# Splitting the top-k search of a 16-expert MoE layer into two groups of eight, the second one run beside the experts

## What is computed

```python
scores = sigmoid(h @ gate_w.T)                       # 2048 x 16, h = layernorm(x1)
cap = ceil(T / E * 2)                                # 256
topk_score, topk_ids = top_k(scores.T, cap)          # per expert: the 256 best tokens
xin = h[topk_ids]
up = einsum(xin, up_w) + up_b; g = einsum(xin, gw) + gb
eo = einsum(silu(g) * up, down_w) + down_b           # hidden width 512
out = zeros.at[topk_ids].add(eo * topk_score)
shared = (silu(x @ sh_gate_w.T) * (x @ sh_up_w.T)) @ sh_down_w.T
return x + out + shared
```

## Time and profile before

| | us |
|---|---|
| median of three runs | 240.09 |
| the three runs | 242.76, 240.09, 237.68 |
| the profiled execution | 242.11 |
| its span | 240.4 |
| PE busy | 195.7 (81%) |
| DVE busy | 129.5 (54%) |
| POOL busy | 105.2 (44%) |
| ACT busy | 76.1 (32%) |
| mean granted TensorE clock | 0.921 |

### The profile page before, as it was taken

How to read it: one execution, slowest core, us unless ns; L and a number is a source line. 1 busy time by engine, 2 the same in 40 slices (tenths; PEclk the granted TensorE clock), 3 DMA queues, 4 the chain that set the end, 5 groups by cost and what they waited for, 6 DMA issues and landing times.

```text
span 240.4 us, 3505 instructions
## 1 busy us (share of the span) xinstructions
PE 195.7 (81%) x1256; PEld 163.0 (68%) x1256; DVE 129.5 (54%) x383; ACT 76.1 (32%) x177; POOL 105.2 (44%) x109
## 2 busy tenths in 40 slices
PE   7579999999697789954979499999999888879100
PEld 7455697999563456543858489989998777769000
DVE  3779167399719999985732434444444443334000
ACT  1475111325955000100021334444444334334100
POOL 7500034146300000000577267877788777635660
PEclk9957999999999999996599979999999999999855
DMA  6999992000008301101042033333233323312331
GB/s 203 387 419 419 414 417 115 3 1 3 1 0 252 121 0 44 46 0 44 17 105 61 14 46 37 46 38 45 37 46 46 50 38 45 26 20 22 24 30 11
DMA packets 11585, 22.20 MB, mean 92 GB/s; under 512 B 1456, under 2 KB 8752, under 8 KB 11440
## 3 DMA queue, kind: packets, MB, share of 16 engines
q1 hardware_dynamic: 5936, 17.52, 19.1%
q0 software_dynamic: 5632, 4.46, 14.3%
HBM read 17.65 MB, written 4.33 MB: 91 GB/s over the span
## 4 chain that ended last, share of the span: by engine, by line
PE 41%; POOL 17%; DVE 13%; DMA 12%; issue 10%; ACT 2%; POOLq 1%; SPq 0%
POOL out_dram L413 10%; DMA out_dram<-area,rows 8%; POOL hT L401 6%; PE bank L1185 5%; PE bank L1186 4%; PE bank L1019 4%; PE bank L1169 4%; PE bank L899 4%; PE bank L920 4%; PE bank L1063 3%; DMA x_tok<-in_x_dram 3%; DVE stats L551 2%; POOL rstd L378 2%; DVE area L746 2%; PE bank L1028 2%
## 5 line engine op out<-in xcount | busy, mean ns | idle before, releaser
L413 POOL DMA_INDIRECT out_dram<-area,rows x32 | 50.8, 1587 | 26.1 <-DMA out_dram<-area,rows 13.0
L401 POOL DMA_INDIRECT hT<-h_rows,rows x32 | 32.5, 1017 | 59.8 <-DVE rows L825 50.3
L530 ACT ACTIVATE sgate<-bank,consts 128x256 f32<-128x256 f32 x64 | 29.9, 469 | 70.9 <-PE bank L1186 60.2
L867 DVE SCALAR_TENSOR_TENSOR area<-bank,consts,sgate 128x256 f32<-128x256 f32 x64 | 30.8, 482 | 39.3 <-ACT sgate L530 32.3
L1185 PE MATMUL bank<-area,wT 128*128 128x256 f32 x128 | 40.1, 395 | 7.7 <-issue 7.0
L1169 PEld LDWEIGHTS bank<-wT,area 128*128 128x128 f32 x256 | 38.6, 193 | 4.2 <-issue 0.9
L1169 PE MATMUL bank<-wT,area 128*128 128x128 f32 x256 | 39.2, 278 | 0.5 <-issue 0.5
L1186 PE MATMUL bank<-area,wT 128*128 128x256 f32 x128 | 38.5, 383 | 0.0
L1186 PEld LDWEIGHTS bank<-area,wT 128*128 128x128 f32 x128 | 24.6, 192 | 3.5
L1185 PEld LDWEIGHTS bank<-area,wT 128*128 128x128 f32 x128 | 19.7, 195 | 10.3 <-issue 9.1
L378 POOL TENSOR_TENSOR rstd<-var_eps,half_pow 128x4 f32<-128x4 f32 (+1 forms) x10 | 12.5, 1249 | 20.7 <-DVE var_eps L556 20.7
(11 more groups left out here) (156 smaller groups left out, 246.8 us busy)
## 6 DMA issues: line engine op xcount, KB each, us to landing
wT<-in_weights_dram SPq DMA_DIRECT2D x16, 768.0 KB, 17.3
h_rows<-hrow SPq DMA_DIRECT2D x2, 576.0 KB, 4.3
x_tok<-in_x_dram SPq DMA_DIRECT2D x2, 512.0 KB, 4.7
x_tok<-in_down_b_dram SPq DMA_DIRECT2D x1, 1024.0 KB, 7.7
out_dram<-x SPq DMA_DIRECT2D x4, 256.0 KB, 2.4
hT<-h_rows,rows POOLq DMA_INDIRECT x32
out_dram<-area,rows POOLq DMA_INDIRECT x32
sh_wT<-in_shared_dram SPq DMA_DIRECT2D x1, 384.0 KB, 6.5
```

The source lines that it names most:

```text
L401: pool.indirect_dma_start(out=gath[:, e % GBUF, c, :], out_offset=None, in_=h_rows[:, :], in_offset=bass.IndirectOffsetOnAxis(ap=rows[:, g ...
L413: pool.indirect_dma_start(out=out_rows, in_=eo[:, e % 2, c, :], in_offset=None, out_offset=bass.IndirectOffsetOnAxis(ap=rows[:, g, c, k:k ...
L530: act.activation(sgate_e[:, q % SGB, :], up_bank(q)[:, CAP:2 * CAP], ACT.Silu, bias=biasT[:, 1, j, e:e + 1]).then_inc(s_sil, 1)
L867: dve.scalar_tensor_tensor(hidden[:, e % 2, j, :], up_bank(q)[:, 0:CAP], biasT[:, 0, j, e:e + 1], sgate_e[:, q % SGB, :], ALU.add, ALU.mul ...
```

## The change

The search, the ranks, the slots and the table are written as functions of a group g of eight experts, with buffers and semaphores of their own for each group (the second group's lie in `diag`, `attn_tok` and bank 7). Group 0 is searched first, with half as many elements in each compare (two of 448), and eight matmuls for a count, since one matmul now takes two tiles; an extra reduction (`total`) adds the two halves. Group 1 is searched later. Its compares are one instruction of 896 elements. Two of its ten rounds stand between `rows[0]` and expert 0, the other eight after the even steps q = 0 to 14; masks, ranks, slots, one-hots and table follow at steps 15 to 24. The shared expert's pieces are dealt out anew: PE does twelve products of them between `positions` and `table`. Bank 7 leaves the up banks, of which four are left. POOL gathers experts 0 to 5 ahead, 6 and 7 before scatters 1 and 2, none before scatters 3 and 4, then 8 and 9 together before scatter 5, and one before each scatter up to the eleventh.

```diff
--- before.py
+++ after.py
-        UP_BANKS = [bank[i] for i in (0, 1, 2, 6, 7)]
+        UP_BANKS = [bank[i] for i in (0, 1, 2, 6)]
...
+        PARTS = (((0, NT // 2), (NT // 2, NT)), ((0, NT),))
+        COUNTS = (bank[5], bank[7])
...
-            for e in range(GBUF - 1):
-                gather(e)
+            got = 0
             for e in range(E):
-                if e + GBUF - 1 < E:
-                    gather(e + GBUF - 1)
+                wanted = e + GBUF if e <= 2 else 8 if e < 5 else min(E, e + 5)
+                for n in range(got, wanted):
+                    gather(n)
+                got = wanted
                 scatter(e)
...
+            def high_keys(g):
+                dve.tensor_scalar(cand[g][:, :, :], ktab[:, :, 0:G], float(1 << ROUNDS[0]), None, ALU.mult)
+                dve.memset(thr[g][:, :], 0.0)
+                link(dve.tensor_scalar(by_tile(bits[g][:, 0, :]), score_bits(g), LOW, None, ALU.arith_shift_right))
+                link(dve.tensor_copy(key[g][:, 0, :], bits[g][:, 0, :]))
+            def low_keys(g):
+                link(dve.tensor_scalar(by_tile(bits[g][:, 1, :]), score_bits(g), (1 << LOW) - 1, None, ALU.bitwise_and))
+                mark(dve.tensor_scalar(key[g][:, 1, :], bits[g][:, 1, :], 1.0, None, ALU.add))
+            def compare(g, r):
+                bit = ROUNDS[r]
+                keys = key[g][:, 2 * (r // len(DIGITS)), :]
+                for i0, i1 in PARTS[g]:
+                    at_c = slice(i0 * G, i1 * G)
+                    dve.tensor_tensor(cmp[g][:, :, at_c].rearrange("p k (i e) -> p k i e", e=G),
+                                      by_tile(keys[:, at_c]).unsqueeze(1).to_broadcast([P, NC, i1 - i0, G]),
+                                      cand[g][:, :, :].unsqueeze(2).to_broadcast([P, NC, i1 - i0, G]),
+                                      ALU.is_ge).then_inc(s_cnt[g], 1)
+                if bit:
+                    dve.wait_ge(s_dve, step[0])
+                    mark(dve.scalar_tensor_tensor(base[g][:, :, :], ktab[:, :, 0:G], float(1 << (bit - 3)),
+                                                  per_expert(thr[g][:, :], NC), ALU.mult, ALU.add))
+            def decide(g, r):
+                bit = ROUNDS[r]
+                dve.wait_ge(s_tot[g], r + 1)
+                link(dve.tensor_reduce(total[g][:, :, :],
+                                       COUNTS[g][:, 0:2 * NC * G].rearrange("p (k s e) -> p k e s", k=NC, s=2), AX.X, ALU.add))
+                link(dve.tensor_scalar(met[g][:, :, :], total[g][:, :, :], float(CAP), float(1 << bit), ALU.is_ge, ALU.mult))
+                link(dve.tensor_reduce(gain[g][:, :], met[g][:, :, :].rearrange("p k e -> p e k"), AX.X, ALU.add))
+                if bit:
+                    n_cand = mark(dve.tensor_tensor(cand[g][:, :, :], per_expert(gain[g][:, :], NC), base[g][:, :, :], ALU.add))
+                    mark(dve.tensor_tensor(thr[g][:, :], thr[g][:, :], gain[g][:, :], ALU.add))
+                    dve.wait_ge(s_dve, n_cand)
+                else:
+                    link(dve.tensor_tensor(thr16[g][:, :], thr[g][:, :], gain[g][:, :], ALU.add))
+                if r == len(DIGITS) - 1:
+                    link(dve.tensor_tensor(above[g][:, :, :], by_tile(key[g][:, 0, :]), per_expert(thr16[g][:, :], NT),
+                                           ALU.subtract))
+                    dve.memset(thr[g][:, :], 1.0)
+                    dve.tensor_scalar(cand[g][:, :, :], ktab[:, :, 0:G], float(1 << ROUNDS[0]), 1.0, ALU.mult, ALU.add)
+                    link(dve.scalar_tensor_tensor(ranked[g][:, :, :], above[g][:, :, :], MARK, by_tile(key[g][:, 1, :]),
+                                                  ALU.mult, ALU.add))
+                    link(dve.tensor_scalar(by_tile(key[g][:, 2, :]), ranked[g][:, :, :], 0.0, MARK, ALU.max, ALU.min))
+            def masks(g):
+                for x, op in enumerate((ALU.is_gt, ALU.is_equal)):
+                    last = dve.tensor_tensor(by_tile(mask[g][:, x, :]), by_tile(key[g][:, 2, :]),
+                                             per_expert(thr16[g][:, :], NT), op)
+                link(last)
...
+            def slots(g):
+                dve.wait_ge(s_pos[g], 1)
+                dve.scalar_tensor_tensor(rank[g][:, 0, :], COUNTS[g][:, 0:P], -UNSET, mask[g][:, 0, :], ALU.add, ALU.mult)
+                link(dve.tensor_tensor(by_tile(rank[g][:, 1, :]), by_tile(COUNTS[g][:, P:2 * P]),
+                                       per_expert(above_no[g][:, :], NT), ALU.add))
+                link(dve.tensor_tensor(rank[g][:, 1, :], rank[g][:, 1, :], mask[g][:, 1, :], ALU.mult))
+                link(dve.scalar_tensor_tensor(slot[g][:, :, :], by_tile(rank[g][:, 0, :]), UNSET, by_tile(rank[g][:, 1, :]),
+                                              ALU.add, ALU.add))
+                dve.tensor_scalar(by_tile(slot_h[g][:, 1, :]), slot[g][:, :, :], HI - 1, None, ALU.bitwise_and)
+                link(dve.tensor_scalar(by_tile(slot_h[g][:, 0, :]), slot[g][:, :, :], 4, None, ALU.logical_shift_right))
...
-                if r in (1, 2):
+                if r == 0:
+                    low_keys(0)
+                elif r in (1, 2):
                     shared_hidden(0, r - 1)
-                elif r in (3, 4):
-                    shared_hidden(1, r - 3)
-                elif r == 5:
+                elif r == 3:
+                    high_keys(1)
+                elif r in (4, 5):
+                    shared_hidden(1, r - 4)
+                elif r == 6:
+                    low_keys(1)
+                elif r == 7:
                     shared_add(0)
-                elif r in (6, 7):
-                    shared_hidden(2, r - 6)
                 elif r == 8:
-                    shared_add(1)
-                elif r == 9:
-                    shared_hidden(3, 0)
-
-            high, low1, both = (key[:, k, :] for k in range(3))
+                    shared_hidden(2, 0)
...
+            high_keys(0)
+            for r in range(len(ROUNDS)):
+                compare(0, r)
                 meanwhile(r)
...
+                decide(0, r)
+            masks(0)
+            count_above(0)
+            shared_hidden(2, 1)
+            slots(0)
...
-            shared_add(2)
+            shared_add(1)
+            shared_hidden(3, 0)
             own_expert(0)
             keep_table(0)
             slot_rows(0)
-            link(one_hot(one_lo, 1, 1))
-            times_token(1)
-            one_hot(one_hi, 0, 1).then_inc(s_hot, 1)
+            compare(1, 0)
+            shared_hidden(3, 1)
+            decide(1, 0)
+            compare(1, 1)
+            shared_add(2)
+            decide(1, 1)
+            compare(1, 2)
             shared_add(3)
...
+            def second_group(q):
+                if q <= 14 and q % 2 == 0:
+                    decide(1, 2 + q // 2)
+                    if q < 14:
+                        compare(1, 3 + q // 2)
+                elif q == 15:
+                    masks(1)
+                elif q == 17:
+                    count_above(1)
+                    slots(1)
+                elif q == 18:
+                    mark(one_hot(one_lo, 1, 1))
+                elif q == 19:
+                    dve.wait_ge(s_dve, step[0])
+                    times_token(1)
+                elif q == 20:
+                    one_hot(one_hi, 0, 1).then_inc(s_hot, 1)
+                elif q == 22:
+                    own_expert(1)
+                elif q == 23:
+                    keep_table(1)
+                elif q == 24:
+                    slot_rows(1)
...
-            own_expert(1)
             dve.wait_ge(s_db_in, 16)
             for q in range(E * FT):
                 e, j = divmod(q, FT)
-                if q == 1:
-                    keep_table(1)
-                if q == 3:
-                    slot_rows(1)
                 dve.wait_ge(s_sil, q + 1)
                 if e >= 2:
                     dve.wait_ge(s_dn, e - 1)
@@ -870,6 +948,7 @@
                     add_bias(e - 1)
                 if j == 2 and e + 1 < E:
                     keep_x(e + 1)
+                second_group(q)
...
+            def count(g, r):
+                for k, (i0, i1) in enumerate(PARTS[g]):
+                    pe.wait_ge(s_cnt[g], len(PARTS[g]) * r + k + 1)
+                    for i in range(i0, i1, 2):
+                        last = pe.matmul(COUNTS[g][:, 0:2 * NC * G], ones_bf[:, :], cmp[g][:, :, i * G:(i + 2) * G],
+                                         start=(i == 0), stop=(i == NT - 2))
+                last.then_inc(s_tot[g], 1)
...
+                if r < 4:
+                    up(1, (0, 2, 1, 3)[r])
+                elif r < 6:
+                    fall(0, 2 * r - 8, 2 * r - 7)
                 else:
-                    up(3, 3)
-                    fall(2, 0, 1)
+                    up(2, (0, 1, 2, 3)[r - 6])
 
             for r in range(len(ROUNDS)):
-                count(r)
+                count(0, r)
                 beside(r)
```

(28 more changed lines are left out.)

201 lines of the change are left out of this document (70 added, 131 removed).

## The result

| | before | after |
|---|---|---|
| median of the runs shown together, us | 241.43 (4 runs) | 249.97 (4 runs) |
| lowest to highest | 237.68 to 242.84 | 247.69 to 251.02 |
| the profiled execution | 242.11 | 249.41 |
| its span | 240.4 | 247.7 |
| mean granted TensorE clock | 0.921 | 0.911 |

The ratio after to before is 1.045, 95% interval 1.029 to 1.061: the changed kernel is slower, by 8.5 us where 1.2 to 2.5 were forecast, and outside the range.

The account below looks back on a forecast made before the run. DVE bounds the search, POOL's work from the first scatter the end. 242.11 less 6.1 gained ahead, plus 4.7 in experts 0 to 6 and 0.6 after scatter 5, gives 241.3; 1.3 of stall makes 242.6 us, range 237 to 248.

Parts of the forecast that it names:

- the term for the stall: ACT's wait before step 4's Silu: at most 4.3 us, 1.3 us put on the change because PE's waits can swallow part.
- The search: Group 0's search on DVE: each round falls by 0.32 us, 3.9 us saved in all.
- The first table: PE's table after the ranks: 0.95 us at full clock for 1.89 us, net 1.1 us saved.
- Rows to expert 0: From first token rows to expert 0: DVE's work takes 7.1 us, just hidden by the first gather's latency.
- Experts 0 to 6: PE and DVE couple through the bias wait: 7.45 us for each of experts 1 to 3, 4.7 us of the gain spent.
- After scatter 5: POOL's end stage: six cycles with a gather and four without, before five and five; 0.6 us more.
- The sum without stall: Whole changed kernel if the stall of step 4 does not come: 241.3 us.
- Before without stall: Whole kernel before if the stall of step 4 does not come: 237.8 us.
- slower by the stall and the clock: Rival, chance 0.22: step 4's stall comes in full on PE's path, with a half-clock expert step; 247.3 us.
- Better overlap: Rival, chance 0.20: PE's own work paces experts 0 to 6; 238.0 us, down to 235.
- The first rows don't come early: Rival, chance 0.08: PE's pieces before the table end late or searches wait on each other; gain ahead 3 us, 244.4.
- DVE loses to POOL: Rival, chance 0.06: compares and one-hots beside gathers wait for them, 4.7 us in all; 246 us.

Follow-up runs that it names:

- a_spread: The changed kernel with four experts gathered ahead instead of six, gathers 2 and 3 held back until keep_x of experts 0 and 1; 241.61 us, ratio 0.997.
- a_nosearch: The changed kernel without rounds 2 to 9 of the second group's search, whose tokens are then not the right ones; 236.62 us, ratio 0.966.
- c_split: s_late_cnt with the first transposes ahead of half of the last shared down products and keep_x(0) ahead of the last shared add; 236.16 us.
- c_split5: The same kernel as c_split, run once more; 237.36 us, ratio 0.981.
- b_pause: The kernel before with one unread power of 128x4 on POOL behind the gathers of experts 1 and 3; 238.73 us, ratio 0.971.
- s_late_cnt: a_spread with DVE's bias one step later and PE's count behind the down product of its step; 236.96 us, ratio 0.974.
- a_four: The changed kernel with four experts gathered ahead instead of six, without waits on gathers 2 and 3; 241.82 us, ratio 0.989.
- c_gates: The changed kernel with all six experts gathered ahead, gathers 2 and 3 waiting for the tokens of experts 0 and 1; 245.53 us, ratio 1.025.
- c_latecnt: The changed kernel with its own gather order, the bias one step later and the count behind the down product; 244.3 us.
- x_tiny: The changed kernel with an added memset of 128x4 on POOL behind the gathers of experts 1 to 4; 248.83 us, ratio 1.035.
- b_late: The kernel before with only its bias one step later; 243.27 us, ratio 1.012.
- b_warm: The kernel before with 38 unread matmuls of 128 columns on PE ahead of its first table; 243.76 us, ratio 1.001.
- x_best: c_split's three edits on the changed kernel's own gather order, with unread powers on POOL behind experts 1 and 3; 236.86 us, ratio 0.980.

## Why the prediction was wrong

The step that failed is the term for the stall: "I put 1.3 us of that on mine", out of a bound of 4.3. x_pause differs from the changed kernel by four powers that nobody reads, which end the stall, and takes 239.2 us for 250.0: 10.8 us between the medians, and 67.2 - 57.9 = 9.3 us at scatter 5 in the profiles, of which 1.1 is the clock's at expert 0 (below). (a_spread gives 8.4.) Both grounds for the low term were wrong.

- *"PE can swallow part"* looked at how long the stall was before and asked what would absorb it. It did not ask what it hangs on. The prediction had noted that POOL's last gather ended at 131.9 and the stall 2 us later, and left it at a "cause I can't name". Read as a dependence, it asks another question: how far does the row reach into the experts? About as far as before (125.9 - 117.9 = 8.0 us of row left when PE starts expert 0, against 131.9 - 122.2 = 9.7), so the stall had to stay, now on a path on which POOL's list no longer covers it. It also caught step 1 and not step 4, and PE reached step 4 129.39 - 117.91 = 11.5 us behind step 0, where the plan has about PE's own 5.46. That is the search's part: in a_nosearch, with no counts between the up products, the first four Silus go through much as in before and the hole stands ahead of step 4 (8.7 us from step 0 to step 4, 8.3 before, 12.4 with the rounds). By the code PE needs nothing back from another engine for steps 0 to 3 there, while with the rounds its count at step 2 needs DVE's compare, which needs the count before.
- *The bound of 4.3 us* was the duration in a kernel where four steps were already through. It was no bound for one where they are not; and half speed followed the stall for 5 us (130 to 135).

The other steps, in the prediction's order:

- *The search*: 2.85 to 2.53 us a round forecast, 2.40 measured. From the first instruction of the search to the first gather, 110.57 - 73.51 = 37.1 us for 115.99 - 71.98 = 44.0: 6.9 us gained for 6.1. The first gather missed 110.0 by 0.6 us only because the search began 1.5 us later in this profile.
- *The first table*: 1.07 us for 0.95, at full clock: right.
- *Rows to expert 0*: 7.1 us forecast, 8.26 measured (117.91 - 109.65). The granted clock was 0.64 from 110.3 to 115.1, and the sum took none of that. In x_pause, where it was 1.00, step 0's Silu stands 7.4 us behind the first gather for 8.5. So this 1.1 us is the clock's; it comes and goes with no change of the code, as 6.7 and 7.6 us in two executions of one kernel show (c_split, c_split5).
- *Experts 0 to 6*: apart from the stall, right in mechanism, and nearly in size. The 7.45 us cycle is 7.2, DVE is busy 0.72 of it and not over 0.8, the bias wait is 1.43 us. Step 4 to the second rows takes 42.9 us for 41.0. Without the stall, x_pause has scatter 5 57.9 us behind the first gather; the plan had 168.75 - 110.0 = 58.75.
- *After scatter 5*: 62 us forecast, 60.9 measured; no other run takes more than 61.5. The reading behind it was a little too even: in before POOL also waits 1.21 us ahead of scatter 1 and 0.96 ahead of scatter 5, and from 207.84 on 2.0 to 3.8 us ahead of each scatter.
- *The sum without stall*, 241.3, against 239.2 (x_pause) and 241.6 (a_spread). *Before without stall*, 237.8, against 238.7 (b_pause). The likes were 3.5 us apart in the forecast; measured they are 0.5 us apart by the medians, and 3.9 by the ratios 0.987 [0.973, 1.001] and 0.971 [0.963, 0.978], whose intervals overlap. No gain of the change by itself shows, and that it costs 3.5 us is not shown either.

Of the rivals, "slower by the stall and the clock" (0.22, 247.3 us) named what happened, and its condition, that both together exceed 3.6 us; it too was 2.7 us short. "Better overlap" needed PE to pace experts 0 to 6, and the bias wait forbade it until s_late_cnt. "The first rows don't come early" is refuted. "DVE loses to POOL" is as well: the compare of 896 takes 0.61 to 0.63 us with a gather beside it and without, so of the rule of the Trainium skill (SBUF — State Buffer, Who interferes with whom), that a VectorE instruction with two SBUF inputs contends with a GpSimd one that reads SBUF, this trace shows nothing on DVE's side. On POOL's side the prediction laid the length of the first two gathers before (1.29 and 1.85 us) to the one-hots beside them; here they take 1.21 and 1.29 us with no one-hot beside, so at most 0.1 and 0.6 us were the one-hots'.

## What to carry to other kernels

A wait in the trace that ends where another engine's activity ends, in run after run, points to a dependence, though no semaphore shows it. Test it by moving that activity, and price a change by where the activity will lie against the work, not by how long the wait lasted before. Where one engine issues a long list of indirect DMAs ahead of need, try breaking the list where other engines need to hand work on: here 4.6 us of idle arithmetic took 10.8 us off one kernel, and some 2 us took 4.1 off the other. And a stall is not worth the same in two kernels (4.1 and 10.8 us here): price it together with the other work that stands on its path.

## What the runs showed of the hardware

- While POOL issues indirect gathers back to back (0.95 us each, 0.30 us between), work that PE has recorded as done reaches ACT late: holes of 2.4 to 4.8 us before a Silu, in most of these runs then two or three Silus at once, and the last Silus that are held start 1.2 to 2.2 us behind the row (before, after, a_four, a_nosearch, c_gates, c_latecnt, x_tiny, b_late, b_warm). Whether the signal is late, or the matmul itself and only its record early, stays open; it wasn't tried. So does whether the issues or their transfers do it, and why single signals get through in a row (four Silus in before and a_nosearch).
- A step of 2.2 us from one issue to the next in place of 1.25 ends it (x_pause, b_pause, x_best); a 0.12 us memset between issues that leaves the pitch at 1.25 us does not (x_tiny).
- The same kernel got a granted clock of 0.72 in one execution and 1.00 in another around the first gathers (c_split5, 110 to 115; c_split, 109 to 114), worth 0.9 us at expert 0; between after (0.75, 109 to 114) and x_pause (1.00) it was 1.1 us.
